# Input and cell gates of a recurrent step: three 16-column products accumulated by TensorE in place of one 16-column and one 32-column product

## The reference

```
def step(carry, xp_t):                       # 256 times, one after the other
    prev_h, prev_c = carry
    h_bar = xp_t + prev_h @ Wh               # Wh: 256 x 1024
    i, f, o = sigmoid(h_bar[:, 0:256]), sigmoid(h_bar[:, 256:512]), sigmoid(h_bar[:, 512:768])
    g = tanh(h_bar[:, 768:1024])
    next_c = f * prev_c + i * g
    next_h = o * tanh(next_c)
```

## Time and profile before

| | us |
|---|---|
| median of 3 runs | 1061.14 (1057.97 to 1061.15) |
| profiled execution | 1060.83 |
| its span | 1058.9 |
| first and last matmul of `lstm_step` at L1409, from the span's start | 41.5 and 638.0 |

### The profile page before, as it was taken

How to read it: one execution, slowest core, us unless ns; L and a number is a source line. 1 busy time by engine, 2 the same in 40 slices (tenths; PEclk the granted TensorE clock), 3 DMA queues, 4 the chain that set the end, 5 groups by cost and what they waited for, 6 DMA issues and landing times. The chain is left out here.

```text
span 1058.9 us, 52234 instructions
## 1 busy us (share of the span) xinstructions
PE 1024.4 (97%) x20286; PEld 932.8 (88%) x20286; DVE 817.9 (77%) x3566; ACT 639.5 (60%) x2495; POOL 284.2 (27%) x864
## 2 busy tenths in 40 slices
PE   5889999999999999999999998999999999999998
PEld 5779999999999999999999986888888888888887
DVE  6678888888888888888888777866666666676797
ACT  4467777777777777777777655333333333343576
POOL 2533343333334333333333301910000000000141
PEclk8758999999999999999999999999999999999999
DMA  8401202211220200000000111000000000000022
GB/s 271 99 28 59 69 25 62 64 47 41 69 68 19 64 24 20 20 19 20 19 4 4 28 15 13 13 2 1 2 2 2 1 2 2 1 4 1 13 86 84
DMA packets 54905, 36.75 MB, mean 35 GB/s; under 512 B 25560, under 2 KB 53514, under 8 KB 54668
## 3 DMA queue, kind: packets, MB, share of 16 engines
q1 hardware_dynamic: 54060, 33.12, 10.8%
q10 hardware_dynamic: 608, 0.30, 0.1%
HBM read 28.42 MB, written 4.98 MB: 32 GB/s over the span
## 5 line engine op out<-in xcount | busy, mean ns | idle before, releaser
L657 ACT ACTIVATE gel<-bank,seq 128x256 f32<-128x256 f32 x256 | 121.2, 473 | 215.4 <-PE bank L1298 211.4
L1296 PE MATMUL bank<-GH,WE 128*128 128x256 f16 x768 | 209.3, 273 | 3.1 <-DVE GH L910 2.2
L1296 PE MATMUL bank<-XHL,WE 128*128 128x256 f16 x768 | 209.2, 272 | 2.7 <-DVE XHL L883 1.2
L1298 PE MATMUL bank<-XHL,WE 128*128 128x256 f16 x768 | 209.5, 273 | 0.0
L1298 PE MATMUL bank<-GH,WE 128*128 128x256 f16 x768 | 209.4, 273 | 0.0
L1297 PE MATMUL bank<-GH,WE 128*128 128x256 f16 x768 | 209.3, 273 | 0.0
L1297 PE MATMUL bank<-XHL,WE 128*128 128x256 f16 x768 | 209.3, 273 | 0.0
L448 POOL TENSOR_TENSOR RH<-rf,RH 128x32 f16<-128x32 f32 x256 | 75.5, 295 | 361.3 <-ACT RH L597 361.2
L1296 PE MATMUL bank<-seq 128*128 128x64 f16 (+2 forms) x1216 | 165.4, 203 | 3.6 <-DVE oz L945 2.4
L1298 PE MATMUL bank<-seq 128*128 128x64 f16 (+2 forms) x1216 | 165.8, 204 | 0.0
L1297 PE MATMUL bank<-seq 128*128 128x64 f16 (+2 forms) x1216 | 165.8, 204 | 0.0
(11 more groups left out here) (216 smaller groups left out, 3079.8 us busy)
## 6 DMA issues: line engine op xcount, KB each, us to landing
stage<-in_L_cond_ew SPq DMA_DIRECT2D x64, 128.0 KB, 2.2
stage<-in_L_cond_W SPq DMA_DIRECT2D x32, 256.0 KB, 3.6
XHL<-in_x SPq DMA_DIRECT2D x8, 512.0 KB, 9.4
out<-WE SPq DMA_DIRECT2D x16, 256.0 KB, 2.1
stage<-in_L_cond_sw SPq DMA_DIRECT2D x2, 1024.0 KB, 5.8
scratch<-rows SPq DMA_DIRECT2D x96, 8.0 KB, 1.9
stage<-in_L_cond_Wx SPq DMA_DIRECT2D x1, 1024.0 KB, 10.0
stage<-in_L_cond_Wh SPq DMA_DIRECT2D x1, 1024.0 KB, 12.1
```

Of the source, the lines that this page charges most:

```text
L657: nc.scalar.activation(gel[:, m % 2, :], banks[m % len(banks)][:, 0:256], ACT.Gelu_apprx_tanh, scale=scale, bias=bias).then_inc(s["a_g"], 1)
L1296: MM(out_, w(HI), x(HI), start=start, stop=False, skip_group_check=True)
L1298: return MM(out_, w(HI), x(LO), start=False, stop=stop, skip_group_check=True)
```

## The change

For input and cell gate, the view `z_ig` loses its second place. Each of the 8 pairs of tile and part now gets three matmuls of 16 columns, all added up in place `a` = 0: LO weights by HI state, HI weights by HI state, and, behind the wait for `v_hl`, HI weights by LO state. The four HI-by-HI matmuls of the forget gate, which stood ahead of the wait for `v_hl`, move behind `pe_ig` and are interleaved with the gate's other two products. The output gate, ScalarE and VectorE are left as they were.

```
                 turn = n // H
                 old = (u + 1) % 2
                 w = lambda h, c, tile: LW[:, h, 1, c, tile * P:(tile + 1) * P]
-                z_ig = IG[turn % 2][:, :].rearrange("p (a m t b) -> p a m t b", a=2, m=NIG, t=H)[:, :, :, u % H]
+                z_ig = IG[turn % 2][:, 0:NIG * H * B].rearrange("p (m t b) -> p m t b", m=NIG, t=H)[:, :, u % H]
...
                 for i, tile in enumerate(IG_TILES):
                     for c in range(C):
-                        MM(z_ig[:, 0, i], w(LO, c, tile), LH[:, old, HI, c], start=False, stop=False,
+                        MM(z_ig[:, i], w(LO, c, tile), LH[:, old, HI, c], start=False, stop=False,
                            skip_group_check=True)
+                        MM(z_ig[:, i], w(HI, c, tile), LH[:, old, HI, c], start=False, stop=False,
+                           skip_group_check=True)
+                if n > 0:
+                    pe.wait_ge(s["v_hl"], n)
+                for i, tile in enumerate(IG_TILES):
+                    for c in range(C):
+                        last = MM(z_ig[:, i], w(HI, c, tile), LH[:, old, LO, c], start=False, stop=(c == C - 1),
+                                  skip_group_check=True)
+                last.then_inc(s["pe_ig"], 1)
                 if u % H == 3 and 2 <= turn < TURNS - 2:
                     pe.wait_ge(s["a_f_seed"], turn - 1)
                 for i, tile in enumerate(F_TILES):
                     for c in range(C):
                         MM(z_f[:, i], w(HI, c, tile), LH[:, old, HI, c], start=False, stop=False, skip_group_check=True)
-                if n > 0:
-                    pe.wait_ge(s["v_hl"], n)
-                for i, tile in enumerate(IG_TILES):
-                    for c in range(C):
-                        last = MM(z_ig[:, :, i], w(HI, c, tile), LH[:, old, :, c], start=False, stop=(c == C - 1),
-                                  skip_group_check=True)
-                last.then_inc(s["pe_ig"], 1)
-                for i, tile in enumerate(F_TILES):
-                    for c in range(C):
                         MM(z_f[:, i], w(LO, c, tile), LH[:, old, HI, c], start=False, stop=False, skip_group_check=True)
                         last = MM(z_f[:, i], w(HI, c, tile), LH[:, old, LO, c], start=False, stop=(c == C - 1),
                                   skip_group_check=True)
```

## The result

The changed kernel took 1098.64 us (median of 4 runs, 1096.32 to 1100.44), before took 1060.85 in the same sessions: ratio 1.0361, interval 1.0331 to 1.0392, so 37.8 us or 3.6% slower. The forecast was 1107.2 with a range of 1096 to 1118: the direction, the mechanism and the range held, the size was 8 us too large. Two executions that ran far longer than the others of their kernel stand in no ratio here: one of before (3549.86 us) and the profiled one of the kernel with sixteen added slots (1919.84 us), of which therefore no profile is read.

A forecast was written before the change was run, and what follows sets the result against it. TensorE's stream was taken to bound 173 of 255 LSTM step ends, the state loop 82. Added slots +52.2, LO-state wait -2.7, VectorE lateness -3.4 gave +46.1 us, hence 1107.2 us, range 1096 to 1118.

The forecast's parts named there:

- TensorE's stream sets the time of the LSTM's steps, the other engines' parts are unchanged: LSTM steps: eight more matmuls per step add 0.204 us, +52.2 us over 256 steps; no other engine's instructions change.
- 25.5 ns a slot, 16 columns as dear as 32, new triples like the old pairs: Small gate matmuls: 25.5 ns start to start, halved columns give nothing back, three matmuls into one place priced like two.
- Weight loads overlap: TensorE: each matmul's weight load overlaps the others, one starting every 25 ns, so only the slot is charged.
- the estimate of 219 us: Eight added weight loads per step paid one behind the other at 107 ns, 0.85 us per step; the prediction rejected it.
- `tf` has no slack, `pe_ig` has: Loop through the engines: `pe_ig` comes 0.10 us later, `pe_f` 0.20; `tf` and all behind it move by 0.20, not 0.10.
- The wait for the low half goes: -2.7: LO-state wait, now behind 16 matmuls instead of 12: all its holes, at most 0.09 us each, vanish, -2.7 us.
- the 110 steps: Steps in which L1420 follows the end of L957 by at most 0.075 us, so TensorE waited for the LO state.
- Second, VectorE ... -3.4: Where VectorE is late by itself, a later `tf` costs nothing; summed step by step, -3.4 us, mostly in blocks 0 and 15.
- the 82 steps bound by the state: Step ends, of 255, where the next step's first matmul starts at most 0.075 us after the end of L952.
- the 173 bound by the stream: The other step ends, set by TensorE's own stream, most with the state ready 0.1 to 0.4 us early; nothing absorbed there.
- the loop gives more back: Rival, chance 0.08: `tf` isn't the late one, loop grows only by `pe_ig`'s 0.10 in 82 steps; +37.9 us, 1099.
- The clock: Rival, chance 0.06: TensorE runs one block more at its lower 1.2 GHz level, large matmuls double; +59 us, 1120.

The follow-up runs named there:

- the kernel with sixteen added slots: Changed kernel plus eight more 16-column zero-data matmuls at the end of each LSTM step, 52 slots per step; 1142.22 us, ratio 1.0771 to before.
- the kernel without the product: Kernel before, input and cell gate without the unread HI-weights-by-LO-state product and its wait, 16 columns, still 36 matmuls; 1056.67 us, ratio 0.9952.
- the run with the old order: Changed kernel with its 44 matmuls, but the forget gate's first four HI-by-HI matmuls again ahead of the LO-state wait; 1097.26 us, ratio 1.0356 to before.
- The pair with 224 slots in two places: Kernel before plus eight zero matmuls ahead of L1391 in blocks 1 to 14: only steps 1 and 9, 1060.70 us; only steps 4 and 11, 1063.50 us.

## Why the prediction came out as it did

- *TensorE's stream sets the time of the LSTM's steps, the other engines' parts are unchanged*: right. Eight zero matmuls that delay no gate cost 32.6 of the 38 us.
- *25.5 ns a slot, 16 columns as dear as 32, new triples like the old pairs*: right. The trace has 25.2; the halved columns gave back nothing (the kernel without the product); the forget gate's triples run at 25.2 ns in the mean over the 256 steps.
- *Weight loads overlap*: right, 25.2 ns from start to start with a load of its own for each matmul. The section "LDWEIGHTS (loading the stationary operand)" of the Trainium skill's page "TensorE: Matmul & The Clock Gate" gives the length of one load, its columns divided by 1.2 GHz; the estimate of 219 us made from it, with the loads paid one behind the other, did not come about.
- *`tf` has no slack, `pe_ig` has*: right. `pe_ig` 0.10 later changed no step. The later `tf` is worth some 3 to 6 us, mostly in block 0 and in blocks 9 to 15.
- *The wait for the low half goes: -2.7*: right in kind, a little short. The waits of the 110 steps add up to 3.5 us when each is taken as in the earlier trace rows. From L1409 to the first matmul of L1437 the mean step grew by 0.19 us (0.83 to 1.02), 49.1 us in all and 47.8 without two single pauses of 1.0 and 0.2, where 52.2 - 2.7 = 49.5 was forecast.
- *"Second, VectorE ... -3.4"*, and nothing else given back behind the gates: here lies most of the miss. Over the 255 step lengths, 47.5 us more in the gates became 37.9 in the steps (both without pauses, by the run with the old order), so some 9.6 came back behind the gates, nearly three times the forecast. Taken by the prediction's own sorting, 3.9 of it lies in the 82 steps bound by the state, where 3.4 was forecast, and 5.7 in the 173 bound by the stream, where nothing was. The step of the working that failed is the sum over the steps bound by the stream: it let TensorE's waits inside a step move along with the rest. Steps 1 and 9 ended 0.1 us or more behind the state and so counted as bound by the stream, but the stream itself held a hole of 0.12 to 0.23 us for GpSimd at L1391; these two steps of blocks 1 to 14 gave back 3.6 us, and the holes at L1391 shrank by 3.5. The pair with 224 slots in two places shows it for L1391. For the holes at `next_x` and at the shared expert it is read from the holes before and after and not tested by a run of its own.
- *The rival "the loop gives more back"* has the very number, 37.9 us and 1099, but not the reason. It rested on `tf` not being the late one, and moving `pe_ig` alone by 0.10 changed no step; and it would have all of the saving in the steps bound by the state, where less than half of it is. That its number fits is luck.
- *The clock*: the rival did not happen; 0.58, 0.95 and 1.00 as before. Block 15 had 0.92 for 0.96, which made its two slow steps 1.8 us longer together in the profiled execution.
- Ahead of the steps, the profiled execution of before had its first L1409 at 41.55, those of the changed kernel and of the nine experiments read between 38.8 and 40.8, so the profile of before is up to 3 us slow in its first part. Behind the last step's start the changed kernel's profile is 1.5 us longer (422.6 against 421.1), with the old order 0.1. Both stand in no step, and the medians are what the comparison goes by.

## What to carry to other kernels

On an engine that the trace shows as busy to 99%, count start to start and subtract the slots: the holes that a pipelined matmul's length hides are what added work can fall into, and what removed work will not give back. For each wait inside the stream ask whether what ends it moves with the added work or hangs on another chain; only the first kind goes on the bill. And a product that nobody reads still costs its wait: leaving out the product and the wait was worth 5 us here (of which the steps of the trace show about 2), putting it to use cost 38.

## What the runs showed of the hardware

- The price of a slot depends on how full this stream is already: 12.6 ns (10.6 to 14.6) for each of the 1024 taken away; for 2048 added at the end of the steps 16 on the kernel before and 21 on the changed one, with the slot itself at 25.2 ns all along.
- At the lower clock level a slot of 16 or 32 columns hardly grows and the large ones double, as the prediction had it: in the kernel before, 48.5 to 65.0 us (granted clock 0.50) has 27, 53 and 107 ns from start to start for 16 or 32, 64 and 128 columns, and the slow steps of block 15 in the changed kernel have 213 for 256, where at 1.00 it is 25, 29, 56 and 108.
- Single pauses of 0.4 to 1.0 us of TensorE that no instruction in the profile ends come in some executions and not in others: 0.9 in block 3 of the kernel before, 1.0, 0.4 and 0.45 in blocks 4, 5 and 7 of the changed kernel, one of 0.8 in block 3 of the same 44 matmuls with the old order. In this kernel they blur one profile's sum by 2 to 3 us; comparing equal steps across blocks takes them out. Each of these five ends 1.4 to 1.6 us after a 16 KB instruction transfer on queue q8 has landed that started 5.4 to 6.7 us after the one before it, where the median distance is 4.3 to 4.5. That TensorE ran short of instructions there is likely by this timing; no run tests it, and other transfers came as late without a pause.
